# The second context attention's loads, cut in halves and spread over four steps

## The reference, cut to what matters

```python
def _L1_xattn_ref(x, latents, mask, Wq, Wkv, Wo, ...):   # x: the context, 12544 x 256
    xn = layernorm(x, ln_x_g, ln_x_b)
    ln = layernorm(latents, ln_l_g, ln_l_b)               # latents: 128 x 256
    q = ln @ Wq
    k, v = jnp.split(jnp.concatenate([xn, ln], axis=1) @ Wkv, 2, axis=-1)
    ...
    sim = jnp.einsum('bhid,bhjd->bhij', q * scale, k) * scale   # 8 heads of 64
    sim = jnp.where(full_mask[:, None, None, :], sim, max_neg)
    attn = jax.nn.softmax(sim, axis=-1)
    ...
```

## Time and profile before

| what | us |
|---|---|
| median of 3 runs | 2588.95 |
| lowest and highest run | 2587.29, 2595.37 |
| the profiled execution's own time | 2589.47 |
| its span, first to last instruction | 2587.8 |

### The profile page before, as it was taken

One profiled execution on the slowest core, in us unless ns is written; L12 is line 12 of the kernel. 1 busy time (PEld: TensorE's weight loads), 2 busy tenths in 40 slices (PEclk: granted clock), 3 DMA queues, 4 the chain that ended last, 5 costly groups with the idle time before them and its releaser, 6 DMA issues. The chain is left out here.

```text
span 2587.8 us, 61939 instructions
## 1 busy us (share of the span) xinstructions
PE 2330.1 (90%) x23416; PEld 1876.8 (73%) x23416; DVE 1800.1 (70%) x4001; ACT 1288.3 (50%) x2509; POOL 728.7 (28%) x907
## 2 busy tenths in 40 slices
PE   8999999999999999967779898989676669999986
PEld 7888888888888888857667776777442258888873
DVE  7888887878888887866876666667552367666615
ACT  5555555545555555526555554555211264555553
POOL 1434224433234342230054554453000010010000
PEclk9999999999999999978889999999677689999996
DMA  7666666666666666538457777776387563444310
GB/s 261 222 237 235 237 224 233 228 243 232 239 238 221 241 234 224 201 138 294 153 198 254 261 261 256 270 257 244 125 337 287 222 203 99 132 130 130 91 47 23
DMA packets 179172, 540.98 MB, mean 209 GB/s; under 512 B 18012, under 2 KB 113456, under 8 KB 172736
## 3 DMA queue, kind: packets, MB, share of 16 engines
q1 hardware_dynamic: 176352, 528.52, 57.6%
q0 software_dynamic: 2304, 8.39, 1.0%
q10 hardware_dynamic: 224, 0.10, 0.0%
HBM read 356.76 MB, written 180.19 MB: 207 GB/s over the span
## 5 line engine op out<-in xcount | busy, mean ns | idle before, releaser
L522 PE MATMUL l0x_psum<-l0x_fast 128*128 128x512 f32 x1764 | 435.7, 399 | 1.6 <-DVE l0x_fast L728 1.0
L522 PEld LDWEIGHTS l0x_psum<-l0x_fast 128*128 128x128 f32 x1764 | 322.3, 188 | 90.3 <-issue 22.1
L640 ACT ACTIVATE l0x_sbuf<-l0x_sbuf 128x896 f32<-128x896 f32 x224 | 251.5, 1126 | 234.9 <-DVE l0x_sbuf L751 234.9
L1839 DVE CUSTOM_DVE_ANT_0 l3x_sbuf<-l3x_psum,key_bias,l3x_sbuf 128x896 f32<-128x896 f32 x224 | 249.2, 1150 | 92.7 <-PE l3x_psum L1683 76.9
L1769 ACT ACTIVATE l3x_sbuf<-l3x_psum 128x512 f32<-128x512 f32 x392 | 221.4, 599 | 179.1 <-PE l3x_psum L1701 172.5
L502 PE MATMUL l0x_psum<-l0x_fast 128*128 128x448 f32 x1344 | 300.1, 372 | 0.0
L751 DVE CUSTOM_DVE_ANT_0 l0x_sbuf<-l0x_psum,l0x_sbuf 128x896 f32<-128x896 f32 x224 | 249.1, 1150 | 21.8 <-PE l0x_psum L537 21.8
L502 PEld LDWEIGHTS l0x_psum<-l0x_fast 128*128 128x128 f32 x1344 | 244.2, 188 | 26.0 <-DVE l0x_fast L734 0.3
L771 DVE STREAM_TRANSPOSE l0x_sbuf<-l0x_sbuf 128x896 f32<-128x896 f32 x224 | 245.9, 1108 | 3.3 <-DMA turns<-l0x_sbuf 2.3
L734 DVE TENSOR_TENSOR l0x_fast<-l0x_psum,l0x_fast 128x448 fp32r<-128x448 f32 x224 | 137.9, 623 | 119.3 <-ACT l0x_fast L613 118.4
L1699 PE MATMUL l3x_psum<-l3x_fast,key_bias 128*128 128x256 f32 x784 | 207.6, 296 | 0.7 <-DVE l3x_fast L1849 0.7
(11 more groups left out here) (778 smaller groups left out, 4209.0 us busy)
## 6 DMA issues: line engine op xcount, KB each, us to landing
turns<-l0x_sbuf SPq DMA_DIRECT2D x112, 896.0 KB, 4.1
l0x_sbuf<-turns SPq DMA_DIRECT2D x112, 896.0 KB, 4.9
turns<-l1x_sbuf SPq DMA_DIRECT2D x56, 896.0 KB, 6.2
l1x_sbuf<-turns SPq DMA_DIRECT2D x56, 896.0 KB, 4.8
last_keys<-ctx_high SPq DMA_DIRECT2D x112, 224.0 KB, 3.4
ahead<-in_L_ffn_W SPq DMA_DIRECT2D x18, 1024.0 KB, 11.4
experts<-in_L_ffn_W SPq DMA_DIRECT2D x18, 1024.0 KB, 12.6
l0x_sbuf<-in_ctxT SPq DMA_DIRECT2D x14, 896.0 KB, 6.9
```

The source lines that it names most:

```text
L522: mm = pe.matmul(ps[:, :], x[:, c, t * T:(t + 1) * T], weights[w][:, c, :], start=(j == 0), stop=(j == len(products) - 1))
L640: act.activation(out, src, ACT.Exp, scale=-1.0, bias=self.negm[:, n % 2, 2 * pr + a:2 * pr + a + 1], accum_out=self.rs[:, m % self.RING, a ...
L1839: dve.tensor_tensor_reduce(junk[:, a, :].rearrange("p (i c) -> p i c", i=2), ps_s[a][:, :, 0:HALF], bias[:, n * CH:(n + 1) * CH].bitcast(F ...
```

## The change

It touches what SP and GpSimd do in this one stage, in chunks 0 to 11. The raw chunk is asked for as two transfers of one feature half each, behind the gathers of steps 0 and 1; the mask as two transfers of half the keys each, behind the gathers of steps 2 and 3. The means of the chunk after move from step 3 to step 2, behind the first half of the mask, and the inverse deviations from step 0 of the next chunk to step 3, behind the second half. Halves have semaphores of their own. GpSimd's norm runs by halves: centre, scale and gain of one half behind the sums of step 0, of the other behind those of step 1. The norm of chunks 0 and 1 stays as it was.

```diff
     def chunk_transfer(self, eng, n, pr):
         s, ahead = self.s, n + 2
-        if self.norm_dram is not None and pr == 0 and ahead < NCH:
-            if n == 0:
-                self.sp_mean(eng, ahead)
-            self.sp_rstd(eng, ahead)
+        if self.norm_dram is not None:
+            self.normed_transfer(eng, n, pr)
+            return
         if pr == 1 and ahead < NCH:
             eng.wait_ge(s.sem("c_low"), 2 * ahead)
             self.sp_raw(eng, ahead)
...
-        if pr == 2 and ahead < NCH and self.mask_dram is not None:
-            eng.wait_ge(s.sem("bias"), ahead)
-            self.sp_mask(eng, ahead)
-        if pr == 3 and ahead + 1 < NCH and self.norm_dram is not None:
-            self.sp_mean(eng, ahead + 1)
...
+    def normed_transfer(self, sp, n, pr):
+        s, ahead = self.s, n + 2
+        if ahead >= NCH:
+            return
+        if n == 0 and pr == 0:
+            self.sp_mean(sp, ahead)
+            self.sp_rstd(sp, ahead)
+        if pr < 2:
+            sp.wait_ge(s.sem("c_low"), 2 * ahead - 1 + pr)
+            self.sp_raw_half(sp, ahead, pr)
+        else:
+            sp.wait_ge(s.sem("bias"), ahead)
+            self.sp_mask_half(sp, ahead, pr - 2)
+        if pr == 2 and ahead + 1 < NCH:
+            self.sp_mean(sp, ahead + 1)
+        if pr == 3 and ahead + 1 < NCH:
+            self.sp_rstd(sp, ahead + 1)
...
+    def sp_raw_half(self, sp, n, c):
+        sp.dma_start(self.raw[:, c, :], self.keysT_dram[:, c, n * CH:(n + 1) * CH]).then_inc(self.s.sem(f"raw_half{c}"), 16)
+
+    def sp_mask_half(self, sp, n, half):
+        lo, hi = half * CH // 2, (half + 1) * CH // 2
+        sp.dma_start(self.raw_mask[:, lo:hi],
+                     self.mask_dram[n * CH + lo:n * CH + hi].partition_broadcast(128)).then_inc(self.s.sem(f"mask_half{half}"), 16)
...
     def norm_center(self, eng, n, c):
-        eng.wait_ge(s.sem("raw_in"), (n + 1) * 16)
+        if n < 2:
+            eng.wait_ge(s.sem("raw_in"), (n + 1) * 16)
+        else:
+            eng.wait_ge(s.sem(f"raw_half{c}"), (n - 1) * 16)
...
     def pool_bias(self, pool, n):
-            pool.wait_ge(s.sem("mask_in"), (n + 1) * 16)
+            if n < 2:
+                pool.wait_ge(s.sem("mask_in"), (n + 1) * 16)
+            for half in range(2):
+                self.wait(pool, f"mask_half{half}", (n - 1) * 16)
...
-            if pr == 1 and self.norm_dram is not None and n + 2 < NCH:
-                self.pool_norm(pool, n + 2)
+            if pr < 2 and self.norm_dram is not None and n + 2 < NCH:
+                self.norm_center(pool, n + 2, pr)
+                self.norm_scale(pool, n + 2, pr)
+                self.norm_gain(pool, n + 2, pr)
```

## The result

The changed kernel takes 2609.28 us (median of 6 runs, 2601.55 to 2615.32), the kernel before 2590.19 in the same comparison (6 runs). The ratio is 1.0081, with a 95% interval of 1.0063 to 1.0099: slower by 19.1 us, where 8.6 us of gain were forecast, and outside the range.

A forecast was written before the change was run, and what follows sets the result against it. Bound taken: a scatter-gather loop, each step as long as gather, context load and scatter in line. Per chunk 9.30 + 8.65 + 9.20 + 9.20 = 36.35 us against 37.21, 8.6 us over ten chunks, giving 2580.4 us; range 2568 to 2598.

The forecast's parts named there:

- the price of 224 KB more in steps 2 and 3: Gather to gather in steps 2 and 3: 672 KB instead of 448 adds 0.88 us each, 8.32 to 9.20.
- the saving in step 1: Gather to gather in step 1: 448 KB instead of 896 cuts 11.27 us to 8.65, saving 2.62.
- a rival for steps 2 and 3 at 0.12: An instruction packet hits the later scatter in steps 2 and 3: 10.08 us each, 2598 us in all; chance 0.12.
- The sum: Four steps of a chunk: 36.35 us against 37.21, 0.86 less; 8.6 us over ten chunks.
- The engines' floor of 8.35: Chunks 12 and 13, without context loads: 8.35 us a step is what the engines need when transfers are light.
- Step 0: First step of a chunk: 448 KB of raw half replaces 448 KB of deviations, so it stays at 9.30 us.
- The extra requests: SP's 24 more requests, some 0.5 us each, fit before the scatter, 2.21 us behind its gather; uncovered, 0.5 a step.
- The fixed part as a rival: Two extra requests a chunk each pay 1.42 us fixed in line: 1.98 us more a chunk, 2608.8 us; chance 0.03.
- The means never held SP: SP's wait for both centrings at step 2: met 1.4 us early; rival that SP is held, chance 0.05.
- The norm by halves: GpSimd's same twelve calls in two pieces, each fitting into a step: cost nothing.
- my own test: Sign of being wrong: steps 2 and 3 at 9.6 us or more, from bytes or code packet.

The follow-up runs named there:

- e4: Changed kernel with the mask written 128 times in device memory, each partition reading its own row, same bytes and requests: 2590.4 us.
- e5: Changed kernel with means and deviations read from rows of their own, mask still shared: steps 2 and 3 take 10.66 and 10.71 us.
- e12: Changed kernel with means or deviations directly behind the gather and the mask half last: steps 2 and 3 take 9.91 and 9.76 us.
- e11: Changed kernel with 128 semaphore increments heading PE's program of the stage, to move the code packets: a chunk takes 39.24 us against 39.16.
- e8: Kernel before with 128 semaphore increments heading PE's program of the stage, to move the code packets: raw step 10.03 us from 11.28, chunk 0.32 shorter.
- e9: Kernel before with the mask kept as bytes, 112 KB at step 2 in place of 448: step 2 of chunk 9 lasts 7.30 us.
- e14: Kernel before with the mask in own rows, in two transfers of 224 KB at step 2: 2591.8 us.
- e3: Kernel before with the shared mask in two halves of 64 partitions, both at step 2: time up 0.4%.
- e2: Kernel before with the shared mask in two halves by keys, both at step 2: 2596.0 us.

## Why the prediction was wrong, point by point

**The step that failed: the price of 224 KB more in steps 2 and 3.** I took 0.88 us from the rate of the raw step's slices, with 0.57 and 1.47 as ends. Measured are 10.68 - 8.52 = 2.16 and 10.20 - 8.43 = 1.77, both outside. The bytes were priced about right: with own rows the same bytes in the same requests cost 0.93 and 1.09 (e4). What I did not price is that all 128 partitions read one row, and that this is slow first behind the gather with another load behind it: 1.23 and 0.68 us by e4, 0.72 in steps without a code packet, whether or not the load behind is shared (e5), and for the larger part a matter of order (e12). It is also the size of the loss: with own rows the kernel is back at 2590.4 us. I had looked at this very thing, and took the rate since the mask behind a gather shows no dip but the longer queue may. It stood alone there, and that says little of it beside another load.

**The second step: the saving in step 1.** Forecast was 8.65 from 11.27, a saving of 2.62; measured 9.39 from 11.28, 1.89. The mechanism was right (e11 has 8.65), but the clean price of the raw chunk's second half is smaller: without a code packet in the way of its scatter the raw step takes 10.03 (e8), so some 1.25 of its 11.28 were a packet in its scatter and not bytes, as far as ten steps of one execution tell. Halving the load does not remove the packets: about three pass in every chunk, three of the changed kernel's ten steps 1 take 9.79 to 10.56 with one, and where e11 clears steps 0 and 1 of them, steps 2 and 3 take the time back (39.24 against 39.16 in a chunk). I had this as a rival for steps 2 and 3 at 0.12, where the step table of before already held the charge.

**The sum.** Forecast per chunk: 0 - 2.62 + 0.88 + 0.88 = -0.86. Measured: -0.23 - 1.89 + 2.16 + 1.77 = +1.81. Times ten this is 18.1; chunk 0 added 3.3 and chunk 11 gave 0.5 back, where I had left both at nothing, and the last two chunks, up to the last gather, gave 2.6 back. The last gather of the stage comes 14.0 us later (1843.95 against 1829.92), and the first came 4.3 earlier; the spans differ by 12.0, and the medians by 19.1, since the profiled execution is the fastest of its kernel.

**The engines' floor of 8.35.** It is a mean over a chunk and not the floor of a step: e9 has steps of 7.30 in a chunk of 36.65. Steps of 448 KB were thus still held by the transfers, and fewer bytes would have paid, which I had not considered.

**What was right.** Step 0 stayed (8.89 against 9.12). The extra requests fit: the scatter follows its gather by 2.21 us in step 2 of chunk 9 (1698.42 - 1696.21) with three requests ahead of it, and by 2.21 in all forty steps of the ten chunks, and e14 shows the second request to be free. The fixed part as a rival is refuted; that its 2608.8 us lies at the measured time is chance. The Trainium skill, DMA: Bandwidth & Descriptors, Rules for kernel authors, advises against two transfers to disjoint partition halves, because they serialize; I applied this to cuts by features and keys. The case of the page is e3, and it agrees that nothing is gained (ratio 1.0038). Cut by keys, a shared row costs 0.35 (e2 against e14), own rows nothing. The means never held SP: they are asked for right behind the mask half in every chunk. GpSimd's timeline has the centring of chunk 9's second half (start, length, operation, idle before):

```profile
1694.11 2.09 POOL L858 TENSOR_TENSOR soon<-soon 128x896 f32<-128x896 f32 x1 [2.46 <-DMA soon<-in_ctxT]
```

It ends 8.7 us behind the gather of step 1 (forecast 8.2), and SP asked for the means at 9.7 (1697.22), right behind the mask half. The norm by halves cost nothing; among the waits it shows only as GpSimd's shorter one for the raw chunk.

By my own test, steps 2 and 3 at 9.6 or more mean bytes or a code packet; it pointed the right way, but neither was the main cause.

**What stays open.** Why a shared row is slow only ahead of another load is not shown: in the changed kernel's hole the engines are 3 to 5 tenths busy, in that of e12 mostly full with slow packets, and what holds them these views don't name. The Trainium skill, DMA: Bandwidth & Descriptors, Latency and other measured facts, tells of copies of 128 partitions between tensors in device memory that fall to about 103 GB/s where the rows lie a large power of two apart, and supposes that the streams meet in one channel of the memory. The rate in most of the hole, 63 to 108 GB/s, is of that size, and rows that coincide would be the extreme case; no run here tells whether that is the mechanism, and by itself it does not say why the row alone costs nothing. Of own rows' 0.93 and 1.09, bytes explain 0.65 (e9) to 0.77 (e8, half of 10.03 - 8.5); the rest may be the means' own shared row or packets, and was not taken apart.

## What to carry to other kernels

Before bytes are moved from one step to another, ask not only how many there are but how they are read: a row spread over all partitions was free alone; between a gather and another load its 224 KB cost 1.8 to 2.2 us in place of 0.9 to 1.1. One kernel with the row written out tells the two apart. A step that is longest in a table may be long by a charge that moves rather than goes; look at what else passes in its transfers before its whole excess is booked as the gain. Where a loop is held by transfers, sending fewer bytes (here a mask of one byte, 10 us) beat every order of sending the same ones that was tried here.

## What the runs showed of the hardware

- A transfer of 224 KB from one shared row, first behind the gather and ahead of another load, left a hole of about 2 us in which 63 to 242 GB/s passed, for the most part 63 to 108; the same bytes from own rows left none. Alone in its step the shared row of 448 KB cost nothing (8.52 against 8.72), and second in line a shared row passed at 308 (e12) and about 400 GB/s (the changed kernel).
- PE's code comes over the same 16 DMA engines (queue q8), 16 KB at a time (192 packets, 3.15 MB in the whole execution), and a packet holds one engine for about 1 us. Steps in which it meets the scatter on which the loop waits are 1.2 us longer than the others in the mean (9.94 against 8.74). The Trainium skill, Runtime: NRT & Kernel Launch, Instruction fetch mechanics, gives this block size and calls the fetch mostly hidden. No row here tells whether PE waits for it; for the transfers on the same engines it was not hidden. The page of the changed kernel has the count:

```profile
q8 instruction: 192, 3.15, 0.5%
```
